# Expert loop in cycles of two steps, three dense quads at its end, and POOL's indirect transfers in bursts per cycle

## What is computed

```python
x = x + _layernorm(_L0_attn_ref(_layernorm(x)))     # 4 S4D layers, x is (16, 512, 128)
# the mixture of experts, on z = _layernorm(x):
probs = softmax(z @ router_w.T)                     # 8 experts
topk_weights, selected_experts = top_k(probs, 2)
for e in range(8):
    ew = sum(topk_weights * (selected_experts == e))
    h = z @ w1[e].T                                 # 128 -> 512
    gate = silu(h[:, :256])
    y = h[:, 256:] * gate @ w2[e].T                 # 256 -> 128
    out = out + y * ew
x = x + _layernorm(out)
```

## Time and profile before

| | us |
|---|---|
| three runs | 1073.33, 1076.9, 1079.39 |
| median | 1076.9 |
| profiled execution, span from the first to the last instruction | 1076.0 |
| of it: PE, DVE, ACT, POOL busy | 724.1, 761.7, 551.7, 521.3 |
| loop's first product begins, last second product ends | 688.2, 1016.8 |

### The profile page before, as it was taken

One profiled execution on the slowest core, in us unless ns is written; L12 is line 12 of the kernel. 1 busy time (PEld: TensorE's weight loads), 2 busy tenths in 40 slices (PEclk: granted clock), 3 DMA queues, 4 the chain that ended last, 5 costly groups with the idle time before them and its releaser, 6 DMA issues.

```text
span 1076.0 us, 25371 instructions
## 1 busy us (share of the span) xinstructions
PE 724.1 (67%) x8523; PEld 611.2 (57%) x8524; DVE 761.7 (71%) x1889; ACT 551.7 (51%) x1197; POOL 521.3 (48%) x704
## 2 busy tenths in 40 slices
PE   0039267794879948795878876677877787787600
PEld 0028267673866658673876655565766676676500
DVE  8978867587675966588675998456555565565697
ACT  7628940188104941079103877333555574565645
POOL 2113224165432654257342766655676626536385
PEclk9999679797988979798988985578999999999955
DMA  7807699963999279982995002211343444444224
GB/s 283 349 1 223 210 385 386 331 243 122 358 340 380 74 258 385 329 299 65 359 386 227 1 11 79 68 36 52 108 125 122 124 120 119 124 117 121 86 82 151
DMA packets 120745, 205.48 MB, mean 191 GB/s; under 512 B 18381, under 2 KB 43481, under 8 KB 119769
## 3 DMA queue, kind: packets, MB, share of 16 engines
q1 hardware_dynamic: 112984, 188.66, 49.5%
q0 software_dynamic: 7680, 15.74, 5.4%
HBM read 167.40 MB, written 36.96 MB: 190 GB/s over the span
## 4 chain that ended last, share of the span: by engine, by line
issue 31%; PE 23%; POOL 20%; DVE 11%; ACT 8%; another core or an unknown queue 2%; DMA 2%; POOLq 1%; SPq 0%; ACTq 0%; DVEq 0%
PE bank L1197 10%; POOL zbuf L614 6%; POOL rstd_of L603 5%; PE bank L1216 4%; POOL toep L696 3%; PE bank L1032 3%; PE bank L1010 2%; ACT glu_work L969 2%; DVE glu_work L1797 1%; POOL sums L594 1%; DMA toep<-kernels_dram 1%; ACT toep L906 1%; ACT glu_work L949 1%; ACT ln_tmp L895 1%
## 5 line engine op out<-in xcount | busy, mean ns | idle before, releaser
L1032 PE MATMUL bank<-zbuf,toep 128*128 128x128 f16 (+3 forms) x3328 | 146.0, 206 | 90.1 <-DVE zbuf L1412 72.2
L1197 PE MATMUL bank<-toep 128*128 128x256 f16 x1248 | 162.2, 283 | 57.0 <-issue 31.0
L1032 PEld LDWEIGHTS bank<-zbuf,toep 128*128 128x128 f16 x3328 | 142.5, 102 | 94.2 <-issue 48.5
L1197 PEld LDWEIGHTS bank<-toep 128*128 (+1 forms) x1248 | 118.3, 101 | 90.5 <-issue 70.2
L614 POOL TENSOR_TENSOR zbuf<-zbuf,w_cur 128x256 f32<-128x256 f32 x120 | 89.7, 749 | 143.0 <-DVE zbuf L1476 142.9
L680 POOL DMA_INDIRECT z_sorted<-toep x120 | 124.2, 1035 | 68.3 <-remote 25.3
L1476 DVE TENSOR_REDUCE zbuf<-bank 128x256 f32<-128x512 f32 x128 | 87.1, 688 | 71.3 <-PE bank L1032 71.2
L1067 PE MATMUL bank<-wo_cur,glu_work 128*128 128x256 f32 x512 | 134.2, 407 | 2.5 <-ACT glu_work L840 2.2
L840 ACT ACTIVATE glu_work<-bank,unscale_cur 128x512 f32<-128x512 f32 x64 | 42.8, 668 | 167.4 <-PE bank L1054 167.3
L1067 PEld LDWEIGHTS bank<-wo_cur,glu_work 128*128 128x128 f32 x512 | 96.3, 198 | 43.4 <-issue 17.8
L1767 DVE SCALAR_TENSOR_TENSOR toep<-bank,toep 128x256 f16<-128x256 f32 x88 | 37.3, 424 | 93.5 <-issue 74.8
(11 more groups left out here) (269 smaller groups left out, 1488.8 us busy)
## 6 DMA issues: line engine op xcount, KB each, us to landing
toep<-kernels_dram SPq DMA_DIRECT2D x104, 1024.0 KB, 14.0
glu_work<-kernels_dram SPq DMA_DIRECT2D x16, 1024.0 KB, 14.1
toep<-z_sorted SPq DMA_DIRECT2D x88, 128.0 KB
y_sorted<-toep SPq DMA_DIRECT2D x88, 128.0 KB
z_sorted<-ln_tmp SPq DMA_DIRECT2D x3, 3072.0 KB, 23.8
toep_last<-kernels_dram SPq DMA_DIRECT2D x8, 1024.0 KB, 14.1
hres<-in_x SPq DMA_DIRECT2D x1, 4096.0 KB, 13.0
toep<-in_x SPq DMA_DIRECT2D x1, 4096.0 KB, 23.9
```

The lines of the kernel that those rows point to most:

```text
L1032: last = MM(dst[:, d * (B // 4):, :], toep_slot(g)[:, c, d * P:(d + 1) * P, k], z_conv[:, 0:QUADS - d * (B // 4), g * GROUP + c].rearrange ...
L1197: last = MM(out[:, piece % 2 * XP:(piece % 2 + 1) * XP], w1_row[:, pw, bass.ds(e + piece * P, P)], xT_s[:, px * XP:(px + 1) * XP], start=( ...
```

## The change

CHOICES and SEGMENTS are cut anew. Quads 3, 14 and 15 are dense; three segments of 12, 20 and 20 tiles need 19, 27 and 27 expert tiles. The loop has 73 sorted steps, now first, then 48 dense ones, whose weights stand at fixed addresses: 121 steps. It is written in cycles of two steps (s, s+1). In a cycle PE transposes the tiles of s+4 and s+5, makes the second products of s−4 and s−3, then the first of s and s+1. ACT does two silus, one copy of 512 columns for two transposed tiles, two high halves and one output of 512 columns for two results; DVE two gatings, one low half of 512 columns, two low halves of inner, and accumulates. The transposed tiles have a ring of 4; x_tile and y_tile lie in the buffer that held the second half of w1 (SP therefore waits for s_wlo), and SP stores 12 tiles behind its loads.

POOL's transfers from number 36 on go in bursts, one per cycle: burst b waits for s_hid ≥ 2b only, then issues 5 scatters (68 are left), or 4 gathers (64, segments 0 and 1), or 3 (40, segment 2). There are 104 scatters and 104 gathers; the first gather of segment 1 is at burst 27 at the earliest, that of segment 2 at burst 40. All gathers are within the loop. Choosing and placing of the last segment, the dense gates, `leads` and the exponents move ahead of the loop, which PE enters after all three segments are placed. In the closing work the gathered pieces come first, the dense ones last.

```diff
-CHOICES = ((0, 12), (12, 20), (32, 16), (48, 16))
+CHOICES = ((0, 12), (12, 24), (36, 20), (56, 8))
...
-DENSE = (3,)
+DENSE = (3, 14, 15)
...
-SEGMENTS = ((0, 12), (16, 16), (32, 16), (48, 16))
+SEGMENTS = ((0, 12), (16, 20), (36, 20))
...
-GATHERED = [(0, 12), (16, 16), (32, 16), (48, 8), (56, 4), (60, 2), (62, 2)]
-PIECES = [(4 * q, 4) for q in DENSE] + GATHERED
+GATHERED = [(0, 12), (16, 16), (32, 4), (36, 12), (48, 8)]
+PIECES = GATHERED + [(4 * q, 4) for q in DENSE]
...
+LOOPED = 8
...
+BURSTS = (5, 5, 4, 3)
...
+            sp.wait_ge(s_wlo, 2)
+            LAG = 12
+            for n in range(0, EXPERT_TILES + LAG + 1, 2):
+                for tile in (n, n + 1):
+                    if tile < EXPERT_TILES:
+                        load(tile)
+                for tile in (n - LAG, n - LAG + 1):
+                    if 0 <= tile < EXPERT_TILES:
+                        store(tile)
...
-            transfers = [0]
-
-            def in_step(stored=None):
-
-
-                d = transfers[0]
-                transfers[0] += 1
-                if d < 36:
-                    if d % 3 == 0:
-                        pool.wait_ge(s_z2T, min(6 + d // 3, QUADS))
-                    return
-                if stored is None:
-                    step, second = (d - 36) // 2 - LEAD, d % 2
-                else:
-                    step, second = stored
-                if 0 < step < STEPS:
-                    if second == 0:
-                        pool.wait_ge(s_hid, step)
-                    else:
-                        pool.wait_ge(s_yps, step - 1)
+            transfers, burst, left = [0], [0], [0]
+
+            def in_burst(size, most):
+
+
+                if left[0] == 0:
+                    burst[0] += 1
+                    pool.wait_ge(s_hid, min(2 * burst[0], most))
+                    left[0] = size
+                left[0] -= 1
...
-                    in_step()
+                    if transfers[0] >= 36:
+                        in_burst(BURSTS[0] if g == 1 else BURSTS[1], (FIRSTS[g] - 6) // 2 * 2 + 2)
+                    elif transfers[0] % 3 == 0:
+                        pool.wait_ge(s_z2T, min(6 + transfers[0] // 3, QUADS))
+                    transfers[0] += 1
...
+                    burst[0] = max(burst[0], (FIRSTS[g] + XTS[g]) // 2 + 3)
...
-                        in_step((DENSE_STEPS + FIRSTS[g] + XTS[g] + 2 + i_g // 2, i_g % 2) if 0 < g < SEGS - 1 else None)
+                        in_burst(BURSTS[3] if g == SEGS - 1 else BURSTS[2], STEPS)
...
+            def xT_high(tiles):
+                first, n = tiles[0], len(tiles)
+                m = first.at % RING
+                if first.at >= RING:
+                    act.wait_ge(s_hid, (first + (n - RING)).n)
+                act.wait_ge(s_xT, (first + n).n)
+                A(xT[:, m:m + n, 0:XP], bank[m // 2].rearrange("p (s n) -> p s n", s=2)[:, 0:n], ACT.Copy,
+                  scale=2.0 * Z_SCALE).then_inc(s_xThi, 1)
+            def y_out(tiles):
+                first, n = tiles[0], len(tiles)
+                m = first.at % RING
+                if first.at >= RING:
+                    for j in range(n):
+                        act.wait_ge(s_yt[m + j], first.div(RING) * 16)
+                A(y_tile[:, m:m + n, :], bank[6 + m // 2].rearrange("p (s n) -> p s n", s=2)[:, 0:n], ACT.Copy,
+                  scale=1.0 / (I_SCALE * W_SCALE)).then_inc(s_yout, 1)
+            def cycle(s):
+                steps = two(s, lambda t: t.is_step)
+                for t in steps:
+                    silu(t)
+                ahead = two(s + EARLY, lambda t: t.is_sorted)
+                if ahead:
+                    xT_high(ahead)
+                if steps and s.at >= LATE:
+                    act.wait_ge(s_yps, (s + (len(steps) - LATE)).n)
+                for t in steps:
+                    inner_high(t)
+                done = two(s + -LATE, lambda t: t.is_sorted)
+                if done:
+                    act.wait_ge(s_yps, (s + (2 - LATE)).n)
+                    y_out(done)
+            cycles(act, cycle)
...
-            pe.wait_ge(s_slots, SEGS - 1)
+            pe.wait_ge(s_slots, SEGS)
...
+                if s.is_sorted:
+                    pe.wait_ge(s_xTsb, s.pair + 1)
+                for t in two(s + EARLY, lambda t: t.is_sorted):
+                    transpose_in(t)
+                for t in two(s + -LATE, lambda t: t.is_step):
+                    second_product(t)
+                for t in two(s, lambda t: t.is_step):
+                    first_product(t)
+            cycles(pe, cycle)
...
-                if q - 10 in LAST_QUADS:
-                    choose(LAST_QUADS.index(q - 10))
-                if q - 12 in LAST_QUADS[:-1]:
-                    places(LAST_QUADS.index(q - 12))
+                if q in PLACE_AT[:SEGS]:
+                    places(PLACE_AT.index(q))
+                if q in CHOOSE_AT:
+                    choose(CHOOSE_AT.index(q))
                 if q - 11 in DENSE:
                     dense_low(DENSE.index(q - 11))
             gates()
-            dve.sem_inc(s_acc, 4)
-
-            def xT_low(n, k):
-
...
+            def cycle(s):
+                steps = two(s, lambda t: t.is_step)
+                for t in steps:
+                    gated(t)
+                ahead = two(s + EARLY, lambda t: t.is_sorted)
+                if ahead:
+                    xT_low(ahead)
+                for t in steps:
+                    inner_low(t)
+                for t in two(s + -LATE, lambda t: t.dense):
+                    accumulate(t)
+            cycles(dve, cycle)
...
-                if i >= len(DENSE):
+                if i < len(GATHERED):
                     dve.wait_ge(s_gath[i], 16 * 2 * n)
-                for t in range(first, first + n) if i >= len(DENSE) else ():
+                else:
+                    dve.wait_ge(s_acc, (i - len(GATHERED) + 1) * 2 * E)
```

276 lines of the change are left out of this document (121 added, 155 removed).

## The result

The changed kernel takes 1110.08 us (median of four runs, 1106.95 to 1111.86) where the kernel before takes 1075.62 beside it: 1.0289 of it, 95% interval 1.0263 to 1.0315. **It is slower by 2.9%.** The forecast was 1102, range 1062 to 1128. The profiled execution's span is 1105.2 us; the sum had 1102.8.

A forecast was written before the change was run, and what follows sets the result against it. The loop was taken as paced by POOL's transfers at 1.5 us each, by PE elsewhere. Loop start 706.7 + 336.6 + 3.9 gave 1047.2; with 55.6 closing work 1102.8, rounded to 1102 us, range 1062 to 1128.

The forecast's parts named there:

- What paces the loop: Expert loop: POOL's count of transfers times 1.5 us wherever it has any, PE elsewhere; 336.6 us in sum.
- the hold: Loop: a burst of n transfers keeps PE's signals from ACT and POOL until 1.46·n us after its start.
- the 0.25 until the next burst: Loop: POOL's next burst begins 0.25 to 0.4 us after the awaited signal; 0.25 was used in the sum.
- the allowance of 2 us for the half clock: First loop stage, 14 bursts of 5: 2 us added for parts at half clock, making 107.7.
- The end of the loop: Last matmul ends at 1047.2 us, 30.4 later than 1016.8.
- The start: Ahead of the loop: PE enters at 697.2, first product at 701, two hidden results seen at 706.7 instead of 704.60.
- Free cycles: Loop cycles without a transfer: 6 before the second segment's rows are stored, 3 before the third's; 39.0 us, then 7.5 dense.
- The closing work: After the last matmul, DVE's: 55.6 us, 3.6 less than before, with exponents and their sum moved ahead of the loop.
- Rival C: Loop: DVE slows bursts too, giving 8.15, 6.75 and 5.25 us for 5, 4 and 3; total 1128.6; chance 0.14.
- Rival A: Loop: signals held only by pairs, not by the burst; POOL back to back at 1.26 us; total 1064.4; chance 0.22.
- what PE signals: Loop: PE's signals during POOL's indirect transfers are seen by ACT and POOL only after the last transfer.
- faster: Whole kernel: chance 0.24 that the change gains time, from Rival A and a small part of another rival.

## Why the prediction was right, point by point

- **What paces the loop.** Right. The step that carried it, 1.46 us held per transfer from the burst's start, was measured at 1.465 for ten, 1.46 to 1.49 for five, and 1.48 to 1.50 for four, and the records of s_hid show the lateness itself. Two terms were a little small, the hold and the 0.25 until the next burst, which is 0.36 to 0.37: together 0.19 more per burst of 5, 0.25 per burst of 4 and 0.06 per burst of 3, some 7 us in all. Against that, the allowance of 2 us for the half clock was not used (the fourteen bursts of 5 took 108.3, for 107.7 with it), and the run began 2.3 us sooner. The end of the loop missed by 2.6. Two things in the reading were too simple: a signal early in a row gets through, and for the sixteen transfers of the earlier trace rows the hold is (700.93 − 678.81)/16 = 1.38 us each, not 1.46.
- **The start.** The first product came 1.7 earlier than said: the count of the 20-tile choice did delay PE's last quad (its last routing begins at 687.95 instead of 685.75, +2.2 where 3.5 were put down), and choice, dense_low and gates did the rest.
- **Free cycles.** 26.1 and 13.7 us of POOL waiting, for 26.4 and 12.6.
- **The closing work.** 55.4 for 55.6, and it stayed DVE's.
- **Rival C (DVE slows a burst)** is out: a burst of five has one or no transfer above 1.1, and its hold keeps to 1.46 to 1.49 a transfer.
- **Rival A** happens, as the whole, on two other chips: nothing is held. The forecast's own run met the hold, as the trace it was made from had, and that is luck: on the other kind of chip the changed kernel takes 1037.7 us, below the range of 1062 to 1128. My price for it was wrong in kind. I set 1064 against a kernel before that had the hold; where nothing is held the kernel before loses it too (987), and the changed one, at 1037.5, is 4.5% slower, not faster. With it the chance given to "faster", 0.24, had no case behind it in anything measured.
- **What was too narrow** is "what PE signals". DVE's signals come late too, beside the row of 51 transfers, and both engines then get single instructions with idle time before each. That cost nothing in this forecast, and more than 20 us in the one for the kernel before with bursts of 3. The expectations called it a lack of new instructions. The trace does not bear that out: the DMA records list the instructions' own queues, and they moved nothing between 982.3 and 1048.8, the stretch in which DVE crawls; the one whose packets are of 16 KB moved nothing between 732.2 and 923.8 in the changed kernel, while PE stalls in every burst. Late signals are what is recorded; what makes them late is not.
- **Size.** The forecast is for one execution's span; the median of runs is 1110, as single runs of both kernels scatter by 0.5%.

Why the change loses, where there is a hold: it takes no transfer's time off the loop. It enters the loop 11 us later, so 36 transfers instead of 42 are out by 704 and six more are left. Its 17 more steps are hidden only beside bursts; in the 16.5 cycles without one they are paid in full. And its bursts hold longer than PE's work of a cycle: 5 · 1.46 and 4 · 1.46 against 4.4. Only the last was tested by itself: bursts of 3 give back 27.6 us in one run and make it equal to the kernel before (1079.39 beside 1075.74). The first two are the forecast's sum, borne out by the loop's end; the run with one dense quad changed several things at once.

## What to carry to other kernels

Count the indirect transfers beside a pipeline, measure what each holds up (here from the distance between a burst's start and the end of the first consumer's "remote" wait), and choose the burst so that what it holds is just under the work that can go on without its signals. A long unbroken row of transfers is not always free cover either: in one case here a pause of 10 us for the other engines shortened the whole. And price a rival's mechanism into both kernels, not into the changed one alone.

## What the runs showed of the hardware

- **One and the same kernel differs by over 8% between sets on different chips.** Before: 990.9 and 992.2 us on two chips; 1075.7, 1080.0 and 1078.5 in three sets on two others. The difference lies beside POOL's indirect transfers: without them in the loop the spans are 1018.6 and 1023.8. Why, the runs don't say. One thing to look at is the recording itself: each run has a profiled span, none was taken without, and where signals are late the trace also lacks records (between 755 and 1004 in the kernel before, 194 of ACT's 325 signals are recorded, and 295 of 302 between 755 and 925 on a chip without the hold). Whether the hold is there when nothing is recorded is open. A comparison holds for a kind of chip: the changed kernel is 1.029 on one and 1.045 on the other, and bursts of 3 are 27.6 us better than its own setting on one kind and 7.5 us slower on the other (spans 1045.0 and 1037.5, on two chips, with PE waiting 20.2 us for loaded tiles instead of 13.6; the intervals of the two ratios touch).
- **Where the hold exists**, the last signal of PE gets through, in nearly every burst, 1.43 to 1.53 us per indirect transfer after the burst's start, for rows of 2, 3, 4, 5, 8, 10 and 12, whether a transfer itself takes 0.95 or 1.3 (1.38 for the row of 16). In a burst of 5 PE gets about 45 matmuls at full pace, in the row of ten 58, then one in about 0.7 us. The Trainium skill, page SBUF — State Buffer, section "Who interferes with whom", knows one such conflict, GpSimd's with DVE; the traces show that one (a transfer of 1.32 beside DVE, 0.95 away from it) and, on at least two chips, this other one, which is much dearer. The same skill, page Runtime: NRT & Kernel Launch, section "Instruction fetch mechanics", has the fetching of instructions mostly hidden; the traces don't speak against it: PE and DVE stall in the two stretches named above, and no such fetch is recorded there.
- **DVE** is hit too, from some 22 us into a row of transfers 1.3 us apart: one instruction in 1.4 us. Beside rows of 32 transfers 1.5 and 1.4 us apart it was hardly hit.
- **A transfer costs POOL 0.96 us with 128 rows and 0.89 with 64**, on a chip without the hold. No run has more rows in a transfer, and none with fewer met the hold; that fewer, larger transfers would pay is a guess from these two numbers.
